# Two mixture-of-experts feed-forward stages of a decoder: every token through every expert, or 39 lists of 128 places each

## The reference

```python
# layer 0, after a root-mean-square norm of the layer-normed x; hidden width 448
top2 of softmax(h @ gate_w.T), their two weights divided by their sum
y = sum over the two experts e: weight_e * ((silu(h @ w1[e].T) * (h @ w3[e].T)) @ w2[e].T)
# layer 2; hidden width 512, with biases, and one more expert ("shared") for every token
top2 of (x @ gate_w + gate_b), softmax over the two
y = sum over the two experts e: weight_e * (gelu(x @ w1[e] + b1[e]) @ w2[e] + b2[e])  + shared(x)
```

## Time and profile before

| what | value |
|---|---|
| median of 3 executions (lowest, highest) | 2977.29 us (2972.89, 2984.81) |
| the profiled execution's own time | 2969.67 us |
| its span in the trace | 2967.9 us |
| mean granted TensorE clock, as a share of full speed | 0.941 |

### The profile page before, as it was taken

The page is one execution under the profiler, slowest core; times in us unless marked ns, Lnnn a source line. Parts: engine busy times, 40 slices in busy tenths (PEclk is TensorE's granted clock), DMA queues, the critical chain, the costliest instruction groups (busy, mean ns, idle before and its releaser), DMA issues. The chain is left out here.

```text
span 2967.9 us, 39202 instructions
## 1 busy us (share of the span) xinstructions
PE 2686.0 (91%) x15208; PEld 1501.1 (51%) x15208; DVE 1767.2 (60%) x2989; ACT 1226.9 (41%) x2546; POOL 1153.4 (39%) x1049
## 2 busy tenths in 40 slices
PE   6999998899979998978788888999999999997899
PEld 3554554656644443446455565466533333334556
DVE  4444435623347771368678777366467888886623
ACT  2333333422216672133355555366534443433422
POOL 2323311365531100052445443099524443442365
PEclk7999998899988999989899999899979999999999
DMA  2000001021110002146222222201000000001032
GB/s 96 1 1 1 1 2 75 1 72 43 57 41 1 1 1 91 44 120 179 71 58 61 76 61 69 97 36 50 0 1 1 1 1 0 1 1 48 2 139 102
DMA packets 34573, 126.46 MB, mean 43 GB/s; under 512 B 9041, under 2 KB 11986, under 8 KB 28466
## 3 DMA queue, kind: packets, MB, share of 16 engines
q1 hardware_dynamic: 32850, 120.79, 12.4%
q0 software_dynamic: 1536, 3.15, 0.5%
HBM read 106.86 MB, written 17.06 MB: 42 GB/s over the span
## 5 line engine op out<-in xcount | busy, mean ns | idle before, releaser
L309 PE MATMUL ps<-parts 128*128 128x512 f32 (+8 forms) x5544 | 1199.6, 431 | 69.6 <-ACT fw_sb L320 16.5
L309 PEld LDWEIGHTS ps<-parts 128*128 128x128 f32 (+3 forms) x5544 | 667.6, 190 | 587.7 <-issue 286.3
L319 ACT ACTIVATE work<-ps 128x512 f32<-128x512 f32 (+5 forms) x954 | 520.0, 571 | 888.7 <-PE ps L309 805.9
L323 POOL TENSOR_TENSOR work<-work 128x512 f32<-128x512 f32 x380 | 512.2, 1364 | 477.5 <-ACT work L319 285.8
L339 DVE TENSOR_REDUCE fw_sb<-ps 128x2 f32<-128x1024 f32 (+3 forms) x384 | 414.6, 1085 | 272.0 <-PE ps L309 271.5
L309 PE MATMUL ps<-work 128*32 128x256 f32 (+5 forms) x2396 | 359.9, 418 | 8.7 <-DVE work L336 4.8
L309 PE MATMUL ps<-work,fw_sb 128*128 128x512 f32 (+1 forms) x720 | 325.6, 551 | 12.4 <-DVE work L323 8.1
L319 ACT ACTIVATE fw_sb<-ps 128x512 f32<-128x512 f32 (+5 forms) x394 | 204.6, 537 | 287.7 <-PE ps L309 247.4
L323 DVE TENSOR_TENSOR work<-work,ps 128x512 f32<-128x512 f32 (+1 forms) x196 | 121.9, 622 | 277.2 <-POOL work L323 271.7
L309 PEld LDWEIGHTS ps<-work 128*32 128x32 f32 (+2 forms) x2396 | 138.2, 137 | 177.7 <-issue 142.2
L313 PE MATMUL ps<-wc_sb,fw_sb 128*128 128x128 f32 x1128 | 203.9, 293 | 12.3 <-POOL fw_sb L336 3.3
(11 more groups left out here) (142 smaller groups left out, 3175.1 us busy)
## 6 DMA issues: line engine op xcount, KB each, us to landing
work<-scr_w SPq DMA_DIRECT2D x29, 1024.0 KB, 4.6
work<-scr_places SPq DMA_DIRECT2D x64, 256.0 KB
work<-scr_sk SPq DMA_DIRECT2D x64, 128.0 KB, 2.6
scr_sp<-wr_sb SPq DMA_DIRECT2D x64, 128.0 KB, 2.2
fw_sb<-in_f SPq DMA_DIRECT2D x1, 6528.0 KB, 18.8
fw_sb<-in_f SPq DMA_DIRECT2D x1, 5376.0 KB, 15.1
fw_sb<-in_f SPq DMA_DIRECT2D x1, 4608.0 KB, 17.6
work<-scr_w SPq DMA_DIRECT2D x8, 512.0 KB, 5.6
```

The source lines that it names most:

```text
L309: return self.e.matmul(o, l, r, start=start, stop=stop) if self.e else Unwritten()
L319: return self.e.activation(o, i, f, bias=bias, scale=scale)
L323: return self.e.tensor_tensor(o, a, b, op) if self.e else Unwritten()
```

## The change

Layers 0 and 2 use a new stage, `Lists`, with routing `ListRoute` (the same chain, then a mask of the chosen pairs). The 4096 pairs of token and expert are laid out expert by expert in places, each expert's list rounded up to whole tiles of 128 places, in at most 39 tiles. `places_dve` adds 35 further instructions on VectorE after the routing weights (36 in layer 2), each but four waiting for the one before: a place for each pair, then a 0/1 matrix `hot` and a table `V`, from whose product (`inverted_pe`, 32 float32 products of 78 columns) come for each tile the numbers of the rows to fetch and to write and the weight of each place, and for each tile the place of its expert's weights in `fw` (`ew`). The tokens are first written, token by token, into an HBM table (`scr_rows`).

Then comes a loop over the 39 tiles. GpSimd fetches the 128 rows of the tile (`fetch_pool`, `gather`); TensorE transposes them; ScalarE copies them from PSUM; TensorE multiplies them as the stationary factor by the weights of the expert, whose column is in a register that `TENSOR_LOAD` has read from SBUF (the `ISA` rows work out addresses from it); activation and product follow, four transposes, four products for down, and ScalarE copies the result with the weight (`output_act`); GpSimd sends the rows to HBM by number (`send_pool`, `scatter`, table `scr_back`). When all are there, SP reads them back and TensorE sums the two rows of each token (`back_pe`). In layer 2 the shared expert runs first, in 16 items of one up and one down product of 512 columns, beside the list making. The weight tensors are packed by expert instead of by unit; the float types of the products are plain float32 throughout.

```diff
-    A = Area(k, parts=2 * T + (4 * 512 + 3 * 1024 if l == 2 else 3 * 512))
-    if l == 0:
-        hT = A.get(T)
-        r = Routing0(k, A, hT)
-        before.append(RootMean(k, "root_mean", hT, r.W.items[1], A.get(16)))
-        units = []
-        for p in range(4):
-            units += [[2 * p]] * 3 + [[2 * p, 2 * p + 1]] + [[2 * p + 1]] * 3
-        return before + [Experts(k, 0, A, r, hT, 14, units, [], 3, 7, ACT.Silu, True)]
-    if l == 2:
-        units = [[u // 4] for u in range(32)] + [None] * 4
-        return before + [Experts(k, 2, A, Routing2(k, A, k.lnT), k.lnT, 0, units, range(32, 36), 0, 9, ACT.Gelu, False, "b1", 3)]
+    if l != 3:
+        A = Area(k)
+        x = A.get(T) if l == 0 else k.lnT
+        big = A.get(4096)
+        r = ListRoute(k, l, A, x, big[:, 0:1024], big[:, 1024:2048])
+        if l == 0:
+            before.append(RootMean(k, "root_mean", x, big[:, 2048:4096], A.get(16)))
+        return before + [Lists(k, l, A, r, x, big)]
+    A = Area(k, parts=2 * T + 3 * 512)
...
+    N = 39
+    def __init__(self, k, l, A, route, x, big):
...
+        self.table = k.dram(f"rows{l}", [2 * T + 1, 128])
+        self.back = k.dram(f"back{l}", [2 * T + 1 + 128 * self.N, 128])
...
+    def inverted_pe(self, e, q):
+        k, t, r, n = self.k, self.tag, self.r, 2 * self.N
+        e.wait_ge(*k.made_v[t, "hot", q])
+        for i in range(8 * q, 8 * q + 8):
+            ins = e.matmul(r.Mb[1][:, 0:n], self.hot[:, tile(i)], self.V[:, n * i:n * i + n], start=i == 0, stop=i == 31)
+        ins.then_inc(*k.summed.up((t, "inverted", q)))
...
+    def shared_pe(self, e):
+        k, t = self.k, self.tag
+        for i in range(16):
+            self.shared_up_pe(e, i)
+            if i == 3:
+                self.prefix_pe(e)
+            if 7 <= i < 11:
+                self.row_pe(e, i - 7)
+            if 10 <= i < 14:
+                self.inverted_pe(e, i - 10)
+            if i > 0:
+                self.shared_down_pe(e, i - 1)
+        self.shared_down_pe(e, 15)
...
+    def turn_pe(self, e, n):
+        k, t = self.k, self.tag
+        e.wait_ge(*self.fetched[n % 4][n])
+        e.wait_ge(*k.made_v[t, "to"])
+        e.wait_ge(*(k.made_a[t, "turned", n - 1] if n or not self.items else k.made_a[t, "shared", 15]))
+        e.transpose(self.XT, self.rows[n % 4], k.cst("id")).then_inc(*k.summed.up((t, "turned", n)))
+    def up_pe(self, e, n, v):
+        k, t, F = self.k, self.tag, self.width
+        e.wait_ge(*k.made_a[t, "turned", n])
+        if self.l == 0:
+            e.wait_ge(*k.made_a[t, "hidden", n - 2])
+            e.matmul(self.G[n % 2][:, 0:F], self.X[n % 3], k.fw[:, bass.ds(v, F)]).then_inc(*k.summed.up((t, "gate", n)))
+            e.wait_ge(*k.made_v[t, "product", n - 2])
+            e.matmul(self.U[n % 2][:, 0:F], self.X[n % 3], k.fw[:, bass.ds(v + F, F)]).then_inc(*k.summed.up((t, "up", n)))
+        else:
+            e.wait_ge(*(k.made_v[t, "biased", n - 1] if n else k.made_a[t, "shared", 15]))
+            e.matmul(self.G[0][:, 0:F], self.X[n % 3], k.fw[:, bass.ds(v, F)]).then_inc(*k.summed.up((t, "up", n)))
+    def down_pe(self, e, n, v):
+        k, t = self.k, self.tag
+        at = self.stride - 512
+        e.wait_ge(*k.made_v[t, "hidden turned", n])
+        e.wait_ge(*k.made_a[t, "output", n - 1])
+        for i in range(4):
+            ins = e.matmul(self.Y, self.FT[n % 2][:, tile(i)], k.fw[:, bass.ds(v + (at + 128 * i), 128)],
+                           start=i == 0, stop=i == 3)
+        ins.then_inc(*k.summed.up((t, "down", n)))
...
+        e.wait_ge(*k.ffn[self.l]["in"])
+        e.wait_ge(*k.made_v[t, "weights at"])
+        v = {0: self.number(e, mybir.EngineType.PE, self.ew[0:1, 0:1], self.stride)}
+        self.turn_pe(e, 0)
+        for n in range(N + 2):
+            if n < N:
+                self.up_pe(e, n, v[n])
+            if n + 1 < N:
+                v[n + 1] = self.number(e, mybir.EngineType.PE, self.ew[0:1, n + 1:n + 2], self.stride)
+                self.turn_pe(e, n + 1)
+            if n >= 2 and self.l == 2:
+                self.down_pe(e, n - 2, v.pop(n - 2))
+            if 1 <= n <= N:
+                self.hidden_pe(e, n - 1)
+            if n >= 2 and self.l == 0:
+                self.down_pe(e, n - 2, v.pop(n - 2))
+        for c in range(NC):
+            self.back_pe(e, c)
...
+    def output_act(self, e, n):
+        k, t = self.k, self.tag
+        e.wait_ge(*k.summed[t, "down", n])
+        e.wait_ge(*k.made_v[t, "to"])
+        e.wait_ge(*self.sent[n % 4][n - 4])
+        e.activation(self.out[n % 4], self.Y, ACT.Copy, scale=self.w[:, n:n + 1]).then_inc(*k.made_a.up((t, "output", n)))
...
+        for n in range(N + 2):
+            if n + 1 < N and self.l == 2:
+                self.turned_act(e, n + 1)
+            if n < N:
+                self.hidden_act(e, n)
+            if n + 1 < N and self.l == 0:
+                self.turned_act(e, n + 1)
+            if n >= 2:
+                self.output_act(e, n - 2)
...
+    def places_dve(self, e):
...
+        of, V = view(self.of, [N, 32], [1, N]), lambda i: view(self.V[:, i * N:], [2 * N, 32], [1, N])
+        each = lambda a: view(a, [1, 32], [0, N])
+        self.step(e, e.tt(of, each(self.j), view(firsts, [0, 32], [1, N]), ALU.is_equal))
+        self.step(e, e.tt(V(0), of, each(k.cst("pairs")), ALU.mult))
+        self.step(e, e.tt(V(1), of, each(self.wk), ALU.mult))
+        for q in range(4):
+            h = view(self.hot[:, 1024 * q:], [128, 8], [1, 128])
+            e.tt(h, view(self.s[:, 8 * q:], [1, 8], [0, 128]), view(seq, [0, 8], [1, 128]), ALU.is_equal
+                 ).then_inc(*k.made_v.up((t, "hot", q)))
...
+    def fetch_pool(self, e, n):
+        k, t = self.k, self.tag
+        e.wait_ge(*k.summed[t, "turned", n - 4])
+        e.gather(self.rows[n % 4], self.table, self.at[:, n:n + 1]).then_inc(*self.fetched[n % 4].up(n))
+    def send_pool(self, e, n):
+        k, t = self.k, self.tag
+        e.wait_ge(*k.made_a[t, "output", n])
+        e.scatter(self.back, self.to[:, n:n + 1], self.out[n % 4]).then_inc(*self.sent[n % 4].up(n))
+    def pool(self, e):
+        k, t, N = self.k, self.tag, self.N
+        for name in ("none", "first", "second"):
+            e.wait_ge(*self.stored[name])
+        e.wait_ge(*k.made_v[t, "places"])
+        for n in range(3):
+            self.fetch_pool(e, n)
+        e.wait_ge(*k.made_v[t, "to"])
+        for n in range(N):
+            if n + 3 < N:
+                self.fetch_pool(e, n + 3)
+            self.send_pool(e, n)
+            if self.l == 0 and 3 <= n < 3 + NC:
+                c = n - 3
+                x = k.xT[:, ch(c)]
+                e.tt(x, x, k.lnT[:, ch(c)], ALU.add).then_inc(*k.made_g.up((t, "sum", c)))
...
+    def sp(self, e):
...
+        for n in range(N - 4, N):
+            e.wait_ge(*self.sent[n % 4][n])
+        for c in range(NC):
+            e.dma_start(view(self.yt[:, 1024 * c:], [256, 4], [1, 256]),
+                        bass.AP(self.back.tensor, 128 * (1 + 1024 * c), [[256, 128], [256 * 128, 4], [1, 256]])
+                        ).then_inc(*self.came.up(c))
```

More of the change, by code:

```diff
@@ L8 @@
 F32R = mybir.dt.float32r
+I32 = mybir.dt.int32
+U32 = mybir.dt.uint32
 ALU = mybir.AluOpType
@@ L65, in layouts @@
                        ("lt4", 128, 16), ("lt8", 128, 64), ("vm2", 128, 128), ("jmask", 128, 4), ("place", 128, 1), ("either", 128, 2),
-                       ("mrow", 128, 1)):
+                       ("mrow", 128, 1), ("seq", 128, 128), ("firsts", 128, 39), ("pairs", 128, 32), ("spare", 128, 39)):
         C.add(name, r, c)
@@ L97, in constants @@
     c["mrow"] = ((i % 32 == 24) | (i % 32 == 25))[:, None] * 1.0
+    c["seq"] = np.broadcast_to(i[None, :], (128, 128))
+    c["firsts"] = np.broadcast_to(128.0 * np.arange(39), (128, 39))
+    n = np.arange(32)[None, :]
+    c["pairs"] = 2 * (128 * (n % 16) + i[:, None]) + n // 16 + 1
+    c["spare"] = 2 * T + 1 + 128 * np.arange(39)[None, :] + i[:, None]
     c["eps5"] = np.full((128, 1), 1e-5)
@@ L223, in pack_inputs @@
     w1, w3, w2 = a["L0_ffn_w1"], a["L0_ffn_w3"], a["L0_ffn_w2"]
-    g = w1.reshape(28, 128, 128).transpose(2, 0, 1)
-    u = w3.reshape(28, 128, 128).transpose(2, 0, 1)
-    d = w2.transpose(0, 2, 1).reshape(28, 128, 128).transpose(1, 0, 2)
-    res["f0"] = np.stack([g, u, d], 2).reshape(128, -1)
+    d = np.concatenate([w2[:, :, 0:384], np.zeros((8, 128, 64)), w2[:, :, 384:448]], 2).transpose(2, 0, 1)
+    d = d.reshape(4, 128, 8, 128).transpose(1, 2, 0, 3).reshape(128, 8, 512)
+    res["f0"] = np.concatenate([w1.transpose(2, 0, 1), w3.transpose(2, 0, 1), d], 2).reshape(128, -1)
     gu, dn = a["L1_ffn_expert_gate_up_w"], a["L1_ffn_expert_down_w"]
@@ L235, in pack_inputs @@
     res["f1"] = np.concatenate([ex, sh], 1).reshape(128, -1)
-    up = np.concatenate([a["L2_ffn_w1"].transpose(1, 0, 2).reshape(128, 32, 128), a["L2_ffn_ws1"].reshape(128, 4, 128)], 1)
```

(28 more changed lines are left out.)

263 lines of the change are left out of this document (added).

## The result

The changed kernel takes 3128.45 us (median of 4 runs, 3114.68 to 3135.14) against 2979.67 us for the kernel before: ratio 1.0495, 95% interval [1.0451, 1.0539], 149 us slower. Forecast were 3180 us, 203 more, with a range of 3030 to 3300. The direction, the mechanism and the range held; the forecast was 52 us too high.

What follows compares the result with a forecast made beforehand. The prediction took both tile loops to be bound by a ring of send, fetch, landing and down products. Layer 0's +95.5 and layer 2's +107.7 us on 2969.7 gave 3173, plus 7.6 to the median: 3180 us, range 3030 to 3300.

Steps and rivals of the forecast that it cites:

- The ring: Tile loops: fetch n+4 waits for send n, tile n+1 for that fetch; 8.3 and 7.7 us a tile; chance 0.62.
- The ring doesn't close: Rival, tile loops: fetched rows come before TensorE needs them, 2.9 and 2.5 us a tile, 2809 us; chance 0.05.
- The landing: Tile loops: a fetch takes 4.40 us from start of issue to usable rows, taken from layer 1, in 70 turns.
- quiet gather: Rival, tile loops: without other traffic a fetch lands in 2.85 us instead of 4.40, total 3072 us; chance 0.18.
- send and gap: Tile loops on GpSimd: the send priced as a gather, 0.95 us, plus 0.30 to the next issue.
- The clock: Tile loops, TensorE: half of the low clock's 1.4 us a turn in layer 0 and 0.95 in layer 2.
- the four sums: Layer 0's tile loop: four sums on GpSimd stand between sends and fetches, 6.3 us.
- The stages' beginnings: Before the loops: layer 0's first fetch at 607 and send 0 at 619.6; layer 2's at 1926.7 and 1938.8.
- The tails: After the loops: last send 4.4 us, read back 5.6, sums 9, last sum and meeting 1.5; 20.5 in layer 2 too.
- The last three tiles: Ends of the loops: three tiles that need no fetch, 5.5 us together in layer 0 and 4.5 in layer 2.
- the register loads and address instructions: Tile loops: priced at nothing, as the pause covers them; uncovered, 39 loads would be 12 us a stage.
- Send in front: Rival, tile loops: a fetch's rows move only after the preceding send's land, 3.45 us a turn, 3421 us; chance 0.12.

Runs made afterwards that it cites:

- the two traffic runs: Changed kernel with SyncE loads beside each tile's send and next fetch, layer 0 alone: one of 1 MB, 3165.15 us; four of 256 KB, 3208.07 us.
- the run with a busy pause: Changed kernel with four unread products of 384 columns on TensorE ahead of each transpose from tile 4 on: 3068.47 us.
- the last run: Kernel with the send two tiles later, plus unread products ahead of layer 0's inversion and both layers' sums, and layer 2's zero row written first: 2849.25 us.
- the two kernels: Kernel with the send two tiles later, with register addresses 2848.18 us, and with constant addresses instead 2847.80 us.
- more instructions: Kernel with the send two tiles later, registers kept, plus six unread 16-column products ahead of each transpose from tile 4 on: 2870.89 us, one run.
- registers: Changed kernel with send n-2 in the place of send n on GpSimd, addresses still in registers: 2848.18 us.
- constants: Kernel with the send two tiles later, with constant weight and bias addresses instead of registers loaded from the list: 2847.80 us.
- the best kernel: Changed kernel with send n-2 in the place of send n on GpSimd: 2848.18 us, ratio 0.9560 to the kernel before.

## Why the prediction was right, and where its sizes were off

**The ring.** Right, and shown: more tiles in it, by order or by buffers, remove the loss. "The ring doesn't close", the rival with the other sign, asked for a landing under 1.5 us behind the start of the issue; it is 2.58.

**The landing is the term that was mis-sized.** The prediction took 4.40 us from layer 1 and named that as its likeliest fault. It is 2.58, measured in the earlier trace rows beside other loads: the "quiet gather" rival was right about it (2.85 by its own sum), and the two traffic runs show that the loads beside it make the difference. The Trainium skill (DMA: Bandwidth & Descriptors, on the anatomy of one DMA from GpSimd) gives 2.15, nearer than my row, 0.4 short. What I held against that rival, the first gather's 3.4 behind its issue, was beside traffic too (197 GB/s). 70 turns of 1.82 too much are 127 us.

**What hid most of that.** A turn of layer 0 at full clock, term by term:

| term | forecast | measured |
|---|---|---|
| transposes to scaled copy (0.11 + 0.44 + 1.05) | 1.60 | 1.70 |
| scaled copy | 0.37 | 0.37 |
| copy to start of send | not priced | 0.27 |
| send and gap | 1.25 | 1.30 |
| start of fetch to transposes | 4.40 | 2.58 |
| sum | 7.62 | 6.22 |

So the hop that I left out and small shortfalls in the send and in TensorE's part gave back 0.42 a turn, 29 us in all. The clock was about right: priced at half of the low clock's cost, 0.7 and 0.5; measured by the run with a busy pause, 0.73 and 0.80, 11 us more in all. The longer landings of some tiles are another 12. With the four sums, all 70 turns were forecast 71 us too long (296.8 us against 254.4 in layer 0, 269.5 against 240.9 in layer 2), where the landing alone would make 127. That the total came within 52 us is therefore partly luck. The quiet gather, right about the landing, gave 3072 and misses by as much on the other side, for it took my other terms as they were.

By the rule of the Trainium skill (TensorE: Matmul & The Clock Gate, on how oscillation of the gate bites) every tile would start at the low clock; the granted 0.81 in layer 0, where turns of 6.2 and of 7.6 us are found, says less often than that: between the two levels 0.5 and 1.0 it means the low one for 38% of the window, and the 0.63 in layer 2 for 74%.

**The stages' beginnings were too short,** by 9 us each: send 0 started 60.0 us into layer 0's stage (forecast 50.8) and 63.5 into layer 2's (54.5). In layer 0 I had counted the last quarter of the inversion at full clock, 1.9 us; all of it ran as one block at low clock (granted 0.50), 13.94, behind 11.08 us in which TensorE was idle. In layer 2 the first fetch stood behind the row of zeros, which VectorE writes only after the list making, and the first transpose behind eight records for the second bias; the last run shows that the second of these is the one that counts. **The tails were shorter** than 20.5 us, 16.2 and 16.8, because the read back begins 2.3 us after the last send starts, not 4.4, and lasts 3.8 up to the sums, not 5.6. The last three tiles took 6.6 and 8.7 us instead of 5.5 and 4.5.

**Priced at nothing, and nearly rightly so:** the register loads and address instructions. Between the two kernels lie 0.4 us, within the noise, and some 8 us in the loops' traces, where GpSimd and TensorE set the pace; in the ring of the changed kernel no run took them out. **"Send in front"** is refuted: a fetch lands 2.58 us after its start with a send 1.3 us ahead and 2.55 with none between copy and fetch.

By stage, forecast less measured is 36.5 us in layer 0 and 19.1 in layer 2, less the 7.2 outside them: 203.2 - 36.5 - 19.1 + 7.2 = 154.8.

## What to carry to other kernels

When one queue issues both the loads and the stores of a tile loop, count the tiles between a store and the load behind it: the loop can't run faster than the whole round (here 6.2 to 7.6 us) divided by that number, whatever the engines' totals say, and moving the store two tiles down the queue was worth 280 us without a byte of memory. Take a transfer's latency from rows with the traffic that will be there: the same gather took 2.6 us alone and 4.3 beside small loads. A pause in each tile also costs clock, so a shorter ring gains more than the time taken out of it (135 us for 90).

## What the runs showed of the hardware that I had not expected

- With GpSimd's issues at their own pace, one tile in two, three or four comes 1.3 to 1.8 us late, the more often the more instructions TensorE has. In the kernel with the send two tiles later VectorE's copy starts 0.03 us after the end of the four transposes in a tile on time, and 2.02 us after it ahead of the late send at 1931.64:

```profile
1923.67 0.60 PE L321 MATMUL ps<-wc_sb,work 128*128 128x128 f32 x4
1924.30 0.69 DVE L344 COPY work<-ps 128x512 f32<-128x512 f32 x1 [0.81 <-PE ps L321]
...
1926.13 0.60 PE L321 MATMUL ps<-wc_sb,work 128*128 128x128 f32 x4
...
1928.75 0.69 DVE L344 COPY work<-ps 128x512 f32<-128x512 f32 x1 [2.79 <-PE ps L321]
```

  The ends of TensorE's records are modelled, so where the 2 us go can't be read from them. One candidate is the loading of instructions. In 100 us of layer 0 the DMA view counts 7, 5 and 4 packets on the instruction queue for more instructions, registers, and constants:

```profile
q8 instruction: 7, 0.11, 0.5%
```

  0.11 MB in 7 packets is 16 KB each. The Trainium skill (Runtime: NRT & Kernel Launch, Instruction fetch mechanics) has instructions refilled in blocks of that size, which agrees, and calls crossing one mostly hidden. But the traces speak against one refill for each late tile: in layer 2's loop there are 6, 5 and 7 such packets (registers, constants, more instructions) for 11, 8 and 16 late tiles, and from 1926 to 1932 us, around the late tile shown, there is none. The cause stays open. The late tiles cost the best kernel about 0.5 us a tile in layer 2, 2.57 against 3.02.
- The form of the traffic matters for an indirect DMA: 1 MB a turn as one load added 1.1 us to a fetch, as four loads that spread one row over 128 partitions 1.7 us.
- A scatter of 128 rows costs GpSimd 0.99 us and a gather 0.97, and neither waits for the other's data: the gather lands in 2.58 us with a scatter 1.3 us ahead and in 2.55 without, the scatter in 2.3 us (median, layer 0) with a gather 1.3 us ahead and without.
